# Layer 1's last stage in pairs of groups, as 64x64 tiles, with x's halves added on the matmul engine

## The reference

```python
zn = _sparse_norm(z, alpha_in, beta_in)            # z is x, group-normalised
a = sigmoid(_lin(zn, W_ga, b_ga)) * _lin(zn, W_la, b_la)
b = sigmoid(_lin(zn, W_gb, b_gb)) * _lin(zn, W_lb, b_lb)
k = einsum('bitc,bjtc->bijc', a, b)
kn = _sparse_norm(k, alpha_o, beta_o)              # mean and variance of all of k
return sigmoid(_lin(zn, W_go, b_go)) * _lin(kn, W_lo, b_lo)      # added to x
```

## Time and profile before

| what | us |
|---|---|
| median of 3 runs (lowest, highest) | 1075.29 (1071.97, 1075.95) |
| the profiled execution's own time | 1071.81 |
| its span in the profile | 1070.0 |
| PE busy | 972.7 (91%) |
| DVE busy | 795.8 (74%) |
| ACT busy | 679.3 (63%) |
| POOL busy | 550.2 (51%) |

### The profile page before, as it was taken

One profiled execution on the slowest core, in us unless ns is written; L12 is line 12 of the kernel. 1 busy time (PEld: TensorE's weight loads), 2 busy tenths in 40 slices (PEclk: granted clock), 3 DMA queues, 4 the chain that ended last, 5 costly groups with the idle time before them and its releaser, 6 DMA issues.

```text
span 1070.0 us, 39570 instructions
## 1 busy us (share of the span) xinstructions
PE 972.7 (91%) x16012; PEld 761.7 (71%) x16012; DVE 795.8 (74%) x1272; ACT 679.3 (63%) x1104; POOL 550.2 (51%) x480
## 2 busy tenths in 40 slices
PE   5689997699999999968999994999999999699997
PEld 5533443598888988957898983878788787555554
DVE  6945788776868768679999997656656465589997
ACT  5758775465656665565777772766758576556664
POOL 0003566781652907416777770854909366145553
PEclk9989999799999999989999996999999999899999
DMA  9900000002113021289989910013040310699994
GB/s 346 357 10 1 2 2 2 2 4 100 62 42 119 4 118 43 70 230 249 220 193 220 206 40 1 4 56 107 4 159 4 102 61 32 180 219 302 290 237 157
DMA packets 173211, 121.96 MB, mean 114 GB/s; under 512 B 69764, under 2 KB 152068, under 8 KB 173064
## 3 DMA queue, kind: packets, MB, share of 16 engines
q1 hardware_dynamic: 173064, 119.73, 41.0%
HBM read 69.38 MB, written 50.33 MB: 112 GB/s over the span
## 4 chain that ended last, share of the span: by engine, by line
PE 69%; DVE 12%; issue 9%; DMA 4%; POOL 2%; ACT 2%; SPq 1%; DVEq 1%; POOLq 0%; ACTq 0%
PE PS L505 61%; DVE WK L1425 4%; DMA AB<-x 3%; PE PS L792 3%; PE PS L824 2%; PE PS L592 2%; POOL AB L360 1%; POOL XT_ALL L1047 1%; DMA AB<-k_scratch 1%; PE PS L519 1%; DVE XT_ALL L1476 1%; SPq L374 1%; DVE WK L1429 1%; ACT WK L922 1%; DVE WK L1349 0%
## 5 line engine op out<-in xcount | busy, mean ns | idle before, releaser
L505 PE MATMUL PS<-EFF,XT_ALL 64*128 64x64 f16 (+1 forms) x11088 | 325.4, 199 | 9.1 <-POOL XT_ALL L1047 3.5
L505 PEld LDWEIGHTS PS<-EFF,XT_ALL 64*128 64x128 f16 (+1 forms) x11088 | 296.1, 96 | 51.2 <-issue 25.6
L505 PE MATMUL PS<-AB 64*128 64x128 bf16 (+2 forms) x2058 | 235.4, 282 | 20.1 <-DVE XT_ALL L1314 7.2
L505 PEld LDWEIGHTS PS<-AB 64*128 64x128 bf16 (+2 forms) x2058 | 197.2, 121 | 58.3 <-DVE XT_ALL L1314 14.1
L922 ACT ACTIVATE WK<-PS,T 128x512 f32<-128x512 f32 x256 | 174.4, 686 | 94.5 <-PE PS L505 82.8
L1111 POOL TENSOR_TENSOR AB<-WK,AB 128x512 f32 x128 | 145.1, 1162 | 110.5 <-ACT AB L932 109.8
L360 POOL TENSOR_TENSOR AB<-WK,MS 128x512 f32 x96 | 130.5, 1390 | 104.9 <-DVE WK L1349 104.9
L1047 POOL TENSOR_TENSOR XT_ALL<-AB,XT_ALL 128x512 f16<-128x512 f32 x60 | 70.9, 1187 | 135.1 <-DVE XT_ALL L1314 131.5
L1121 POOL TENSOR_TENSOR WK<-XT_ALL 128x512 f32 (+1 forms) x64 | 73.8, 1156 | 84.1 <-PE PS L777 58.6
L1357 DVE TENSOR_TENSOR WK<-PS,WK 128x512 f32<-128x512 f32 x128 | 85.7, 687 | 32.5 <-ACT WK L922 32.5
L1349 DVE TENSOR_TENSOR WK<-PS,WK 128x512 f32<-128x512 f32 x128 | 86.7, 689 | 30.6 <-ACT WK L922 23.9
(11 more groups left out here) (195 smaller groups left out, 1552.3 us busy)
## 6 DMA issues: line engine op xcount, KB each, us to landing
AB<-x SPq DMA_DIRECT2D x64, 512.0 KB, 6.6
p_scratch<-WK SPq DMA_DIRECT2D x32, 512.0 KB, 2.6
k_scratch<-WK SPq DMA_DIRECT2D x64, 256.0 KB, 2.1
AB<-k_scratch SPq DMA_DIRECT2D x32, 512.0 KB, 9.6
out<-AB SPq DMA_DIRECT2D x16, 1024.0 KB, 7.0
AB<-p_scratch SPq DMA_DIRECT2D x29, 512.0 KB, 7.9
AB<-p_scratch SPq DMA_DIRECT2D x2, 640.0 KB, 5.7
AB<-spread SPq DMA_DIRECT2D x1, 896.0 KB
```

The source lines that it names most:

```text
L505: return nc.tensor.matmul(dst, lhsT, rhs, start=start, stop=stop)
```

## The change

- z, gate and x's halves go by pairs of groups. `pair_matmuls` issues, for each pass, four matmuls, one for each group b of the pair and each parity q: the 64 rows of parity q, 64 weight columns, written to the 64 PSUM partitions `(q ^ b) * 64` of bank `bank + b`. The parities of the second group thus come out swapped, and its transposes multiply by `swapped`, the identity with its halves exchanged, to put them back.
- The sum of x's halves is made by PE: `pair_sums` multiplies both halves by a 64x64 identity in float16 (`eyes`) and adds them up in banks 2 and 3. DVE's second instruction reads that from PSUM and writes `x1out`. POOL has no work in the stage. Gates now have banks 0 and 1, the sums 2 and 3, z 4 and 5, the transposes 6 and 7.
- The last chunk projects one pair of gates and one pair of sums ahead, in place of four gates.
- DVE's order is y, y, o, o; ACT's sigmoid, sigmoid, copy, copy.
- `k_scratch` is laid out `[CH, 2, ROWS, P]`, parity outside the row. `store_k` becomes two DMAs a channel with runs of 512 B; `load_k` reads runs of 8 KB.
- `swapped` and `eyes` are made by four DVE copies after `biases_ready`, ahead of layer 1's products.

```diff
-    k_dram = nc.dram_tensor("k_scratch", [CH, ROWS, 2, P], f32, kind="Internal").ap()
+    k_dram = nc.dram_tensor("k_scratch", [CH, 2, ROWS, P], f32, kind="Internal").ap()
...
-                    sp.dma_start(k_dram[ds(at_c, 1), :, :, :].rearrange("c (h m) q p -> m c h (q p)", h=2),
-                                 st1[:, c % 4].rearrange("m (h n) -> m h n", h=2).unsqueeze(1)
-                                 ).then_inc(k_stored[c % 4], 16)
+                    tile = st1[:, c % 4].rearrange("m (h q p) -> m q h p", h=2, q=2)
+                    for q2 in range(2):
+                        sp.dma_start(k_dram[ds(at_c, 1), q2, :, :].rearrange("c (h m) p -> m c h p", h=2),
+                                     tile[:, q2].unsqueeze(1)).then_inc(k_stored[c % 4], 16)
...
+                def pair_matmuls(bank, j, passes):
+
+                    for i, (w, at, x) in enumerate(passes):
+                        for b in range(2):
+                            for q in range(2):
+                                rows = slice(q * CH, (q + 1) * CH)
+                                to = slice((q ^ b) * CH, (q ^ b) * CH + CH)
+                                last = mm(PS[to, bank + b, :], w[rows, at[q]:at[q] + CH], x(2 * j + b)[rows, :],
+                                          i == 0, i == len(passes) - 1)
+                    return last
+
+                def pair_gates(j):
+                    at = E_G, E_G + CH
+                    pair_matmuls(0, j, ((w_hi, at, lambda g: half(g, 0)), (w_lo, at, lambda g: half(g, 0)),
+                                        (w_hi, at, lambda g: half(g, 1)))).then_inc(gate1_done, 1)
+
+                def pair_sums(j):
+                    pair_matmuls(2, j, [(eyes, (0, 0), lambda g, i=i: half(g, i)) for i in range(2)]
+                                 ).then_inc(x1sum_done, 1)
...
+                        pe.wait_ge(prod_done[layer], q * NP + (NP - 3))
+                        pair_gates(0)
+                        pe.wait_ge(prod_done[layer], q * NP + (NP - 2))
+                        pair_sums(0)
...
+                    for j in range(NG // 2 + 1):
+                        if j < NG // 2:
+                            b = 2 * j // PG1
+                            if 2 * j % PG1 == 0:
+                                pe.wait_ge(kt_in[b % PS1], 32 * (b // PS1 + 1))
+                            reached(pe, y1_done, 2 * j)
+                            tile = kt[:, b % PS1, :].rearrange("p (g n) -> p g n", n=BANK)
+                            pair_matmuls(4, j, ((EFF, (E_Z, E_Z + CH), lambda g: tile[:, g % PG1, :]),)
+                                         ).then_inc(z1_done, 1)
+                        if j + 1 < NG // 2:
+                            pe.wait_ge(gate1_ready, 2 * j + 2)
+                            pair_gates(j + 1)
+                        if j > 0:
+                            pe.wait_ge(o_done, 2 * j)
+                            if j < NG // 2:
+                                pair_sums(j)
+                            reached(pe, ob_ready, 2 * j - 2)
+                            for b in range(2):
+                                g = 2 * j - 2 + b
+                                for r in range(GR):
+                                    last = nc.tensor.transpose(PS[:, 6 + b, r * P:(r + 1) * P],
+                                                               x1out[:, g % 4, r:BANK:GR], swapped if b else ident)
+                                last.then_inc(back_done, 1)
...
-            def x1_sum(g, k):
-                reached(pool, back_done, g - 3)
-                nc.gpsimd.tensor_tensor(x1sum[:, k % 4], half(g, 0), half(g, 1), ALU.add).then_inc(x1sum_done, 1)
...
+                    def outputs(g0, pair, j):
+                        dve.wait_ge(z1_done, pair + 1)
+                        for k in (2 * j, 2 * j + 1):
+                            dve.wait_ge(gate1_ready, g0 + (k + 1))
+                            V.scalar_tensor_tensor(gate1[:, k % 4], PS[:, 4 + k % 2, :], col(34), gate1[:, k % 4],
+                                                   ALU.add, ALU.mult).then_inc(y1_done, 1)
+                        dve.wait_ge(x1sum_done, pair + 1)
+                        reached(dve, back_done, g0 + (2 * j - 2))
+                        for k in (2 * j, 2 * j + 1):
+                            dve.wait_ge(y1_done, g0 + (k + 1))
+                            V.scalar_tensor_tensor(x1out[:, k % 4], PS[:, 2 + k % 2, :], col(24), gate1[:, k % 4],
+                                                   ALU.mult, ALU.add).then_inc(o_done, 1)
...
+                    dve.wait_ge(pn_done_p, NG)
+                    for q in range(2):
+                        step(V.tensor_copy(swapped[:, q * CH:(q + 1) * CH], ident[:, (1 - q) * CH:(2 - q) * CH]))
+                        rows = slice(q * CH, (q + 1) * CH)
+                        step(V.tensor_copy(eyes[rows, :], ident[rows, rows]))
```

More of the change, by code:

```diff
@@ L227, in build @@
         rstd2 = S1[:, :].rearrange("p (q r) -> p q r", q=2)
+        swapped = S1[:, 0:P]
+        eyes = S1[:, P:P + CH // 2].bitcast(f16)
         ident_in = sem("ident_in")
@@ L450, in _ @@
                         if b + PS1 < NB1:
-                            sp.wait_ge(z1_done, (b + 1) * PG1)
+                            sp.wait_ge(z1_done, (b + 1) * (PG1 // 2))
                             load_k(b + PS1)
@@ L694, in chunk @@
                             project(q + 1, n)
-                    else:
+                    elif layer == 0:
                         for g in range(AHEAD):
@@ L759, in _ @@
                     pe.wait_ge(weights_ready, 2)
[L760 to L779, removed]
@@ L967, in _, with gate1_pairs @@
                 if layer == 1:
[L968 to L974, removed]
+                    def gate1_pairs(g0, pairs, evictions):
+                        for j in pairs:
+                            for k in (2 * j, 2 * j + 1):
+                                if k % 2 == 0:
+                                    act.wait_ge(gate1_done, g0 // 2 + (j + 1) if isinstance(g0, int)
+                                                else pair0[0] + (j + 1))
+                                reached(act, o_done, g0 + (k - 3))
+                                nc.scalar.activation(gate1[:, k % 4], PS[:, k % 2, :], ACT.Sigmoid,
+                                                     bias=T[:, 32:33], scale=T[:, 28:29]).then_inc(gate1_ready, 1)
                             if evictions:
-                                evict(g - 4, k - 4)
+                                evict(g0 + (2 * j - 4), 2 * j - 4)
+                                evict(g0 + (2 * j - 3), 2 * j - 3)
                     def evict(g, k):
@@ L1112, in _ @@
                                                 ALU.subtract).then_inc(ablo_done, 1)
-            for s in range(4):
-                pool.wait_ge(k_stored[s], 16 * (CH // 4))
-            pool.wait_ge(acc_done, 2 * CH)
-            def x1_sum(g, k):
-                reached(pool, back_done, g - 3)
-                nc.gpsimd.tensor_tensor(x1sum[:, k % 4], half(g, 0), half(g, 1), ALU.add).then_inc(x1sum_done, 1)
-            for k in range(8):
-                x1_sum(k, k)
-            with pool.Fori(1, NG // 8) as i:
-                for k in range(8):
-                    x1_sum(i * 8 + k, k)
         @block.vector
@@ L1420, in _ @@
                     final(V.tensor_tensor(col(34), PS[:, 7, 4:5], col(33), ALU.add), weights_ready, 2)
[L1422 to L1434 removed]
+                    def outputs(g0, pair, j):
[6 more added lines that the diff above has]
+                        reached(dve, back_done, g0 + (2 * j - 2))
+                        for k in (2 * j, 2 * j + 1):
+                            dve.wait_ge(y1_done, g0 + (k + 1))
+                            V.scalar_tensor_tensor(x1out[:, k % 4], PS[:, 2 + k % 2, :], col(24), gate1[:, k % 4],
+                                                   ALU.mult, ALU.add).then_inc(o_done, 1)
+                    for j in range(4):
+                        outputs(0, j, j)
+                    with dve.Fori(1, NG // 8) as i:
+                        for j in range(4):
+                            outputs(i * 8, i * 4 + j, j)
                     break
```

39 lines of the change are left out of this document (13 added, 26 removed).

## The result

| | us |
|---|---|
| before, median of 4 runs (lowest, highest) | 1073.78 (1071.97, 1075.95) |
| after, median of 4 runs (lowest, highest) | 1056.01 (1055.50, 1059.29) |
| ratio, 95% interval | 0.9827 (0.9801 to 0.9853) |
| the profiled execution after, and its span | 1059.29, 1057.4 |

The change makes the kernel 1.7% faster, 18 us. The forecast was 1049 within 1037 to 1066.

The account below looks back on a forecast made before the run. PE's stream was taken as full at 1.98 us a group, DVE full too. First z 935.0 plus 106.4, plus 4.85 and 1.8, gave 1048.1 profiled, 23.7 less; median forecast 1049, range 1037 to 1066.

Parts of the forecast that it names:

- change of shape: PE switching between 64-row tiles and 128-row transposes: 0.10 us each, two a pair, 0.20.
- lag of the weight loads: Tiles' weight loads at a burst's head come in turn, so the fourth ends late: 0.12 us, bounds 0 and 0.46.
- first product: First z of the last stage starts at 935.0, bounds 934.1 and 936.5, against 936.06 before.
- first product to last copy: Last stage: 31 steps of 3.20 = 99.2, last pair's own way 6.2, start at the lower clock 1.0; sum 106.4 us.
- the likeliest case: Four tiles, column halves included, stream together on PE; kernel at 1043 to 1054 us, chance 0.48.
- the worst case: Column halves on PE don't overlap at all: 5.0 us a pair, 1104; within the 0.11 for wholly unhidden weight loads.
- Weight loads are hidden: Rival on PE's tiles: loads not hidden, 4.35 us a pair, 1084, chance 0.11; half of it 3.65, 1062, chance 0.13.
- hand-made schedule: One pair followed from z at 0: DVE about 2.8, ACT 2.74 at most, under 3.2; PE sets the pace.
- The gates taken ahead: Before the last channels of k, gates ahead drop from 4 groups to 2 and a sum: cost 0.
- the load's runs grow: k load ahead of the first z: runs from 512 B to 8 KB should bring the first block sooner; at most 2 us.
- The stores of k: 512 B runs instead of 1 KB, twice the DMAs, while k's channels run: cost 0, without much cover.
- DMA in the stage: Last stage's 33.6 MB at 300 GB/s done at 1040, keeping up; rival that DMA becomes the bound: 1057, chance 0.09.

Follow-up runs that it names:

- POOL's relief: Kernel before, with POOL's sum of x's halves covering only the first 64 of 512 columns: 0.9982 of the kernel before.
- second trace: Trace from running the unchanged kernel after once more, beside the old k layout: span 1049.0 us.
- spoiling them: Kernel after, with each pair's second group on the same two quadrants as the first, transposes using the plain identity: 1.0361 of the kernel before.
- the old runs: Kernel after with k's old layout (parity inside the row, 512 B load runs, one store a channel): 0.9847, then 1062.72 us, 0.9866 of the kernel before.
- the second set: The unchanged kernel after run once more, beside the old k layout: 1053.90 us, 0.9791 of the kernel before.
- the first set: The first runs of the kernel after, against the kernel before: median 1056.01 us, 0.9827.
- the one-load kernel: Kernel after with k's parity outermost, one DMA loading each block to all 128 partitions instead of two to 64: 1053.5 us, 0.9792 of the kernel before.
- the first filler: One-load kernel with the pair of sums taken ahead repeated four more times before the last channels of k: 1050.9 us, 0.9763 of the kernel before.
- relieving the other alone: Kernel after with POOL's sums and DVE's two SBUF inputs back, PE's own sums removed: 1.0092 of the kernel before.

## Why the prediction was right

The mechanism held for the steady period, which is nearly all of the gain; two steps ahead of the first product failed. The terms, the forecast beside what the traces have:

| term | forecast | measured |
|---|---|---|
| bound of the kernel before | PE, DVE level with it | so: POOL's relief gives 0.2% |
| product, four tiles | 0.86 | 0.91 |
| gates | 0.65 | 0.65 |
| sums on PE and the change of shape behind them | 0.43 + 0.10 | 0.54 |
| eight transposes and the change of shape behind them | 0.94 + 0.10 | 1.16 |
| lag of the weight loads | 0.12 | in the rows above |
| period of a pair | 3.20 | 3.26 |
| o from PSUM | 0.74, 0.70 in step | 0.74, 0.70 |
| first product | 935.0 | 936.8 in the second trace |
| first product to last copy | 106.4 | 107.6, 107.4 |
| against before, profiled | 23.7 less | 21.0 less (second trace) |

- **Tiles.** The unknown, column halves, came out as the likeliest case had it, and spoiling them gives 5.20, the 5.0 of the worst case. Weight loads are hidden: eight float32 loads of 64 columns in 0.21 us and twelve float16 ones without a gap in the stream. In place of the lag that I put at 0.12 the trace has 0.17 in two places, 0.05 in the product and 0.12 in the first four transposes behind the change of shape (0.59 against 0.47).
- **The others at that period.** DVE idles 0.55 us a pair and ACT 0.84; the hand-made schedule leaves 0.4 and 0.5. That DVE's new instruction would be free of POOL was priced by its form and shown by keeping POOL busy.
- **The first product** was late by 1.8 us. Two steps failed. "The gates taken ahead ... that part of PE ends before it waits for POOL's halves of k: 0" was 1.5 to 1.6: the longer idle costs the clock. And "the load's runs grow ... which should bring the first block sooner": it landed in 6.8 to 6.9 us instead of 7.6, with 64 partitions at a time (4.80 with 128).
- **First product to last copy.** In the second trace 31 x 3.26 = 101.1 and 6.3 for the two ends; the forecast had 99.2 and 7.2. So the period was 1.9 us short in all, and ends priced 0.9 too high hid half of that.
- **The stores of k** with 512 B runs cost nothing in the pace of the channels: the second and third chunks take 21.93 and 21.94 us in the traces after. **DMA in the stage** kept up, as forecast, at 357 GB/s for the 322 needed. With the old runs it was the bound. The prediction counted the new layout for little beyond the first load; it is worth 8 to 9 of the second set's gain of 24 us.
- The absolute number, 1049, lies 7 below the median of the first set and 5 below that of the second (1053.9, whose before was 1077.7). The share of the gain, 23.7 forecast, is 17.8 in the first set and 23.8 in the second; both intervals are about 3 us to each side. That the second set meets the forecast to 0.1 is luck: by the traces the change gives 2.7 us less than forecast, 1.8 at the first product and 1.0 in the stage.

The best of the versions run is the one-load kernel with the first filler, 0.9763: 2.4% under before, ahead of the kernel after by 0.6% of the first set, where the intervals don't meet, and by 0.3% of the second, where they do; the two weren't run side by side.

## What to carry to other kernels

When two engines are both full at one period, the chain of waits names one of them; here relieving that one alone bought 0.2%, and relieving the other alone, in the new order of work, lost 0.9%. Half-zero weights on a 128x128 array are worth cutting into four 64x64 tiles if each tile of a pass has its own quadrant: product and gates went at about half their cost, for 0.2 us of shape changes a pair and 0.12 in the transposes behind one. And work moved out of an engine's waiting time isn't free if that work was what kept its clock up.

## What the runs showed of the hardware

- Four 64x64 tiles of 512 columns take about what one full-width matmul takes (0.65 against 0.65 for three float16 passes, 0.91 against 0.86 for the float32 product); on two quadrants double (1.30, 1.77).
- Two DVE instructions with two SBUF inputs next to two POOL sums take 3.03 to 3.10 us, about 1.5 beside sums cut to 64 columns (0.75 each). Even tiny ones suffer: the first small scalar_tensor_tensor after the statistics took 1.07 us beside POOL and 0.22 with POOL idle. DVE's way from the statistics to the last small result was 8.05 us before (925.96 to 934.01) and 8.68 in the kernel after with POOL kept busy (932.25 to 940.93); with POOL idle it was 6.32 and 6.42 (935.55 to 941.87, 927.21 to 933.63).
- Loads with 8 KB runs go at 426 GB/s to 128 partitions and at 217 to 229 to 64 at a time (windows of 2 and 4 us in the two traces of the kernel after and the one with POOL busy).
- Ahead of the last channels of k PE was idle for 1.22, 1.22, 1.45, 1.45 and 1.87 us in five traces, and the channels ran at 2.4 GHz in 21.9 us; it was idle for 2.93 or 2.94 us in six and 3.36 in one, and each time the clock fell to 1.2 GHz for a while and they took 23.4 to 23.5 us.
